# A graph network's edge loop: source buckets rounded up to single tiles, and node weights split in quarters in the loop and behind it

## What is computed

```python
edge_index = jnp.stack([src, dst])
h = jnp.maximum(_layernorm(x), 0.0)
# first layer, row = src, col = dst
edge_feature = silu(edge_rbf @ We1 + be1) @ We2 + be2     # 20625 x 512
msg = edge_feature * h[col]
agg = segment_sum(msg, row, num_segments=625)
x = x + h + (silu(agg @ Wn1 + bn1) @ Wn2 + bn2)
...
# later layers use the same edges, summed by either end, as dense 625 x 625 sums
```

## Time and profile before

| what | value |
|---|---|
| median of 3 runs (lowest, highest) | 1288.35 us (1287.68, 1288.88) |
| profiled execution | 1288.21 us |
| its span on the core | 1286.5 us |
| mean granted clock of TensorE | 0.966 of full speed |
| busy: PE / DVE / ACT / POOL | 93% / 66% / 53% / 37% of the span |

### The profile page before, as it was taken

One profiled execution on the slowest core, in us unless ns is written; L12 is line 12 of the kernel. 1 busy time (PEld: TensorE's weight loads), 2 busy tenths in 40 slices (PEclk: granted clock), 3 DMA queues, 4 the chain that ended last, 5 costly groups with the idle time before them and its releaser, 6 DMA issues.

```text
span 1286.5 us, 21145 instructions
## 1 busy us (share of the span) xinstructions
PE 1200.5 (93%) x6356; PEld 1000.9 (78%) x6356; DVE 855.2 (66%) x1433; ACT 684.9 (53%) x1349; POOL 469.6 (37%) x570
## 2 busy tenths in 40 slices
PE   6989799999999999999999999977879999897687
PEld 4668688888888888888888888867668798876576
DVE  8676377777777777777777777764655171453752
ACT  3475576666666667666666666664423141313241
POOL 2002555555555555555555555613211020221200
PEclk9989899999999999999999999997989999998978
DMA  5533522222222222222222222211001020111101
GB/s 209 210 132 140 207 82 75 71 80 82 80 78 74 74 82 82 79 73 72 82 82 80 78 70 79 80 35 42 1 34 66 1 82 16 39 61 33 42 1 40
DMA packets 27295, 97.22 MB, mean 76 GB/s; under 512 B 6541, under 2 KB 6791, under 8 KB 22906
## 3 DMA queue, kind: packets, MB, share of 16 engines
q0 software_dynamic: 19040, 55.73, 14.5%
q1 hardware_dynamic: 8218, 40.98, 8.8%
HBM read 87.83 MB, written 8.85 MB: 75 GB/s over the span
## 4 chain that ended last, share of the span: by engine, by line
PE 84%; DVE 8%; ACT 4%; issue 3%; DMA 1%; POOL 0%; DVEq 0%; SPq 0%; ACTq 0%
PE ps L821 12%; PE ps L820 12%; PE ps L822 12%; PE ps L813 9%; PE ps L814 9%; PE ps L815 9%; PE ps L914 3%; PE ps L915 3%; PE ps L827 3%; PE ps L828 3%; PE ps L866 2%; PE ps L919 2%; PE ps L854 1%; PE ps L1045 1%; DVE zb_lo L1534 1%
## 5 line engine op out<-in xcount | busy, mean ns | idle before, releaser
L820 PE MATMUL ps<-we_hi,s_hi 128*128 128x512 f32 x680 | 276.7, 407 | 1.8 <-ACT ps L642 1.8
L821 PE MATMUL ps<-we_lo,s_hi 128*128 128x512 f32 x680 | 269.8, 397 | 0.0
L822 PE MATMUL ps<-we_hi,s_lo 128*128 128x512 f32 x680 | 268.1, 394 | 0.0
L483 POOL DMA_INDIRECT xg<-h_dram,node_picks x170 | 178.1, 1048 | 99.2 <-POOL node_picks L473 67.9
L477 POOL DMA_INDIRECT rbf<-in_edge,edge_picks x170 | 175.3, 1031 | 51.8 <-issue 28.6
L639 ACT ACTIVATE m_hi<-msg 128x512 fp32r<-128x512 f32 x170 | 107.6, 633 | 146.9 <-DVE msg L1374 146.9
L1367 DVE TENSOR_TENSOR s_lo<-s,s_hi 128x1024 fp32r<-128x1024 f32 x85 | 104.2, 1226 | 82.9 <-ACT s_hi L633 82.9
L1379 DVE TENSOR_TENSOR m_lo<-msg,m_hi 128x512 fp32r<-128x512 f32 x170 | 117.8, 693 | 58.6 <-ACT m_hi L639 58.6
L822 PEld LDWEIGHTS ps<-we_hi,s_lo 128*128 128x128 f32 x680 | 127.6, 188 | 31.1
L820 PEld LDWEIGHTS ps<-we_hi,s_hi 128*128 128x128 f32 x680 | 128.0, 188 | 26.2 <-issue 2.0
L821 PEld LDWEIGHTS ps<-we_lo,s_hi 128*128 128x128 f32 x680 | 128.8, 189 | 23.0
(11 more groups left out here) (254 smaller groups left out, 2584.6 us busy)
## 6 DMA issues: line engine op xcount, KB each, us to landing
stage<-in_fold_a SPq DMA_DIRECT2D x6, 1024.0 KB, 5.7
stage<-in_fold_b SPq DMA_DIRECT2D x6, 1024.0 KB, 8.6
fold_dram<-folded SPq DMA_DIRECT2D x6, 1024.0 KB, 5.6
wstage<-fold_dram SPq DMA_DIRECT2D x6, 1024.0 KB, 5.0
w_raw<-in_nodew SPq DMA_DIRECT2D x3, 1024.0 KB, 11.0
wstage<-in_selfw SPq DMA_DIRECT2D x3, 1024.0 KB, 4.8
rbf<-in_edge,edge_picks POOLq DMA_INDIRECT x170, 2.7
xg<-h_dram,node_picks POOLq DMA_INDIRECT x170, 3.5
```

The lines of the kernel that those rows point to most:

```text
L483: pool.indirect_dma_start(xg[t.slot][:, j], None, h_dram, bass.IndirectOffsetOnAxis(ap=node_picks[t.slot][:, j:j + 1], axis=0)).then_inc(x ...
L820: pe.matmul(outp, lh, rh, start=False, stop=False, skip_group_check=True)
L821: pe.matmul(outp, lh, rl, start=False, stop=False, skip_group_check=True)
L822: return pe.matmul(outp, ll, rh, start=False, stop=False, skip_group_check=True)
```

## The change

The buckets are rounded up to single tiles of 128 slots. TILES = (20625 + 5 * 127) // 128 = 166, so 83 steps. The even part of each bucket's tiles goes, as pairs, first; the odd tiles left over (at most five) are put behind, from position `solo_at`, at step 80 (SOLO) or later. Steps 80, 81 and 82 may then hold two tiles of different buckets, so each of their tiles has its own sum (banks 5 and 7 for the aggregate, 6 and 0 for the pairs) and its own flush: 86 flushes in all. `whole(c)` counts the flushes before step c, and waits in these steps are on those counts. The sort gets the operations that put the last odd tile of a bucket at its place (`limit`, `jump`, an additional pass over `rank`), and the bucket table has nine passes instead of four.

The node weights are no longer split in the last three steps. w[0] is split by quarters (128 x 512) in steps 1, 2, 80 and 81 on ACT and one step later on DVE, with a semaphore of its own for its transfer. w[1] and w[2] are split whole behind the loop: on ACT after the five copies of the turned aggregate, on DVE after the five low parts. TensorE waits for w[0] before the aggregate is turned, and for the other two before `mlp2`.

The diff without declarations, in which lines of context are left out too:

```diff
@@ -28,8 +28,11 @@
 PAIR = 2 * P
-STEPS = (E + C * (PAIR - 1)) // PAIR
-TILES = 2 * STEPS
+TILES = (E + C * (P - 1)) // P
+STEPS = TILES // 2
+SOLO = STEPS - (C + 1) // 2
+FLUSHES = 2 * STEPS - SOLO
+WEIGHT_CHUNKS = {1: 0, 2: 1, SOLO: 2, SOLO + 1: 3}
...
@@ -107,6 +110,11 @@
+
+def whole(c):
+    return c + max(0, c - SOLO)
...
@@ -355,10 +371,17 @@
-        WEIGHTS = ((we2_hi, we2_lo, we2_raw), (we1_hi, we1_lo, we1_raw),
-                   *((w_hi[i], w_lo[i], w_raw[i]) for i in range(3)))
+        WEIGHTS = ((we2_hi, we2_lo, we2_raw), (we1_hi, we1_lo, we1_raw))
+        NODE_WEIGHTS = len(WEIGHTS) + len(WEIGHT_CHUNKS)
+        def scattered(eng, t):
+            if t.reg is None and t.c > SOLO:
+                eng.wait_ge(scat_mm, 2 * whole(t.c - 1))
+            else:
+                t.wait(eng, scat_mm, 2, -2)
...
@@ -398,13 +421,14 @@
             for i in range(3):
-                sp.dma_start(w_raw[i][:].rearrange("p k f -> p (k f)"), a["nodew"][i]).then_inc(node_weights_in, 16)
+                sp.dma_start(w_raw[i][:].rearrange("p k f -> p (k f)"), a["nodew"][i]).then_inc(
+                    first_weights_in if i == 0 else node_weights_in, 16)
-            sp.wait_ge(flushed, STEPS)
+            sp.wait_ge(flushed, FLUSHES)
...
@@ -571,10 +595,7 @@
                 for i in range(start, end):
-                    if i < 2:
-                        act.wait_ge(edge_weights_in, 32)
-                    else:
-                        act.wait_ge(node_weights_in, 48)
+                    act.wait_ge(edge_weights_in, 32)
...
@@ -644,7 +665,7 @@
                 act.wait_ge(hots_ready, t.count(3, 1))
-                t.wait(act, scat_mm, 2, -2)
+                scattered(act, t)
...
@@ -656,6 +677,12 @@
             def pairs_high(t):
+                if t.reg is None and t.c >= SOLO:
+                    for j in range(2):
+                        act.wait_ge(scat_mm, 2 * whole(t.c) + 3 + j)
+                        act.wait_ge(flushed, whole(t.c) - 1 + j)
+                        act.activation(pairs_i[j][:, 0:ND], ps[0:NC, 6 - 6 * j, 0:ND], ACT.Copy).then_inc(pairs_out, 1)
+                    return
...
@@ -675,8 +702,10 @@
                     seed(1)
-                if t.reg is None and t.c >= STEPS - 3:
-                    weights_high(t.c - STEPS + 5, t.c - STEPS + 6)
+                if t.reg is None and t.c in WEIGHT_CHUNKS:
+                    k = WEIGHT_CHUNKS[t.c]
+                    act.wait_ge(first_weights_in, 16)
+                    act.activation(w_hi[0][:, k], w_raw[0][:, k], ACT.Copy).then_inc(weights_hi, 1)
...
@@ -697,9 +726,12 @@
-            act.wait_ge(flushed, STEPS)
+            act.wait_ge(flushed, FLUSHES)
+            act.wait_ge(node_weights_in, 32)
+            for i in range(1, 3):
+                act.activation(w_hi[i][:], w_raw[i][:], ACT.Copy).then_inc(weights_hi, 1)
...
@@ -909,6 +941,17 @@
                 pe.wait_ge(oh_src_ready, t.count(1, 1))
+                if t.reg is None and t.c >= SOLO:
+                    pe.wait_ge(agg_flushed, whole(t.c))
+                    for j in range(2):
+                        pe.matmul(ps[0:NC, 5 + 2 * j], oh_src[s][:, j, 0:NC], m_hi[s][:, j], start=True, stop=False)
+                        pe.matmul(ps[0:NC, 5 + 2 * j], oh_src[s][:, j, 0:NC], m_lo[s][:, j],
+                                  start=False, stop=True).then_inc(scat_mm, 1)
+                    pe.wait_ge(pairs_out, whole(t.c))
+                    for j in range(2):
+                        pe.matmul(ps[0:NC, 6 - 6 * j, 0:ND], oh_srcb[s][:, j, 0:NC], oh_dst[s][:, j, 0:ND],
+                                  start=True, stop=True).then_inc(scat_mm, 1)
+                    return
...
@@ -992,10 +1035,10 @@
-            pe.wait_ge(flushed, STEPS)
-            pe.wait_ge(weights_hi, len(WEIGHTS))
-            pe.wait_ge(weights_lo, len(WEIGHTS))
-            turn("aggT", lambda c, k: agg3[:, c, k * P:k * P + P], flushed, STEPS, 0)
+            pe.wait_ge(flushed, FLUSHES)
+            pe.wait_ge(weights_hi, NODE_WEIGHTS)
+            pe.wait_ge(weights_lo, NODE_WEIGHTS)
+            turn("aggT", lambda c, k: agg3[:, c, k * P:k * P + P], flushed, FLUSHES, 0)
...
@@ -1017,6 +1060,8 @@
+            pe.wait_ge(weights_hi, NODE_WEIGHTS + 2)
+            pe.wait_ge(weights_lo, NODE_WEIGHTS + 2)
...
@@ -1236,18 +1281,34 @@
             dve.wait_ge(rank_mm, 2)
-            link(dve.tensor_scalar(total_i[:], ps[:, 0, TOTAL_AT:TOTAL_AT + C], float(PAIR - 1), None, ALU.add))
-            shift_by = PAIR.bit_length() - 1
-            link(dve.tensor_scalar(chunks_i[:], total_i[:], shift_by, None, ALU.logical_shift_right))
-            link(dve.tensor_copy(chunks_f[:], chunks_i[:]))
-            link(dve.tensor_tensor_scan(upto[:], chunks_f[:], zeros5[:], 0.0, ALU.add, ALU.add))
+            link(dve.tensor_scalar(total_i[:], ps[:, 0, TOTAL_AT:TOTAL_AT + C], float(P - 1), None, ALU.add))
+            link(dve.tensor_scalar(tiles_i[:], total_i[:], P.bit_length() - 1, None, ALU.logical_shift_right))
+            dve.tensor_scalar(half_tiles[:, 0], tiles_i[:], 1, None, ALU.logical_shift_right).then_inc(halved, 1)
+            dve.tensor_scalar(half_tiles[:, 1], tiles_i[:], 1, None, ALU.bitwise_and).then_inc(halved, 1)
+            dve.wait_ge(halved, 2)
+            link(dve.tensor_copy(chunks_f[:], half_tiles[:]))
+            for i in range(2):
+                link(dve.tensor_tensor_scan(upto[:, i], chunks_f[:, i], zeros5[:], 0.0, ALU.add, ALU.add))
-            link(dve.scalar_tensor_tensor(out=offset[:], in0=first[0:EP], scalar=float(PAIR), in1=ps[0:EP, 0, RANK_AT:RANK_AT + C],
+            dve.tensor_scalar(limit[:], upto[:, 0], float(PAIR), None, ALU.mult).then_inc(halved, 1)
+            dve.tensor_scalar(solo_at[:], upto[:, 0, C - 1:C], float(SOLO), float(PAIR), ALU.max, ALU.mult).then_inc(halved, 1)
+            dve.wait_ge(halved, 3)
+            dve.scalar_tensor_tensor(out=jump[0][:], in0=first[:, 1], scalar=float(P), in1=limit[:],
+                                     op0=ALU.mult, op1=ALU.subtract).then_inc(halved, 1)
+            link(dve.scalar_tensor_tensor(out=offset[:], in0=first[0:EP, 0], scalar=float(PAIR), in1=ps[0:EP, 0, RANK_AT:RANK_AT + C],
+            dve.wait_ge(halved, 5)
+            dve.tensor_scalar(jump[1][:], jump[0][:], solo_at[:, 0:1], None, ALU.add).then_inc(halved, 1)
-            dve.wait_ge(rows_part, 3 * C + 3)
+            dve.wait_ge(halved, 6)
+            for b in range(C):
+                dve.wait_ge(rows_part, 2 * C + 4 + b)
+                dve.tensor_scalar(member[:, b], rank[:, b], limit[0:EP, b:b + 1], jump[1][0:EP, b:b + 1],
+                                  ALU.is_gt, ALU.mult).then_inc(halved, 1)
+            dve.wait_ge(halved, 6 + C)
+            link(dve.tensor_tensor(rank[:], rank[:], member[:], op=ALU.add))
...
@@ -1299,13 +1360,17 @@
                 dve.wait_ge(consts_ready, 9)
-                link(dve.tensor_scalar(first_tile[:], first[:], 2.0, None, ALU.mult))
-                link(dve.tensor_scalar(bucket_f[0][:], tile_no[:], first_tile[:, 1:2], None, ALU.is_ge))
-                for b in range(2, C):
-                    link(dve.scalar_tensor_tensor(out=bucket_f[(b + 1) % 2][:], in0=tile_no[:], scalar=first_tile[:, b:b + 1],
-                                                  in1=bucket_f[b % 2][:], op0=ALU.is_ge, op1=ALU.add))
-                link(dve.tensor_scalar(tile_base[:], bucket_f[C % 2][:], float(NC), None, ALU.mult))
-                link(dve.tensor_copy(bucket_row[:], bucket_f[C % 2][0:1, 0:TILES:2]))
+                link(dve.tensor_scalar(pairs_end[:], upto[:, 0], 2.0, None, ALU.mult))
+                link(dve.tensor_scalar(solo_tile[:], solo_at[:], 1.0 / P, None, ALU.mult))
+                link(dve.tensor_scalar(solo_end[:], upto[:, 1], solo_tile[:, 0:1], None, ALU.add))
+                link(dve.tensor_scalar(bucket_f[0][:], tile_no[:], solo_tile[:, 0:1], float(1 - C), ALU.is_ge, ALU.mult))
+                ends = [pairs_end[:, b:b + 1] for b in range(C - 1)] + [solo_end[:, b:b + 1] for b in range(C - 1)]
+                for i, end_at in enumerate(ends):
+                    link(dve.scalar_tensor_tensor(out=bucket_f[(i + 1) % 2][:], in0=tile_no[:], scalar=end_at,
+                                                  in1=bucket_f[i % 2][:], op0=ALU.is_ge, op1=ALU.add))
+                bucket = bucket_f[len(ends) % 2]
+                link(dve.tensor_scalar(tile_base[:], bucket[:], float(NC), None, ALU.mult))
+                link(dve.tensor_copy(bucket_row[:], bucket[0:1]))
...
@@ -1393,7 +1458,16 @@
-                b = dve.value_load(bucket_row[0:1, bass.ds(t.count(1), 1)], min_val=0, max_val=C - 1)
+                if t.reg is None and t.c >= SOLO:
+                    buckets = [dve.value_load(bucket_row[0:1, t.count(2, j):t.count(2, j) + 1], min_val=0, max_val=C - 1)
+                               for j in range(2)]
+                    for j, b in enumerate(buckets):
```

(22 more changed lines are left out.)

26 lines of the change are left out of this document (17 added, 9 removed).

## The result

The changed kernel takes 1258.69 us (median; 1257.98 to 1259.49), the kernel before 1288.51 in the same comparison: 0.977 of its time, 95% interval 0.976 to 0.979. The profiled execution took 1257.98 us with a span of 1256.1, 30.4 less than the span before.

A forecast was written before the change was run, and what follows sets the result against it. TensorE, 100% busy in the loop, was taken as the bound. Terms -16.87 (steps), -7.6 (loop end), -0.9 (placing matmuls), +0.3 (start) took 1288.21 us to 1263.2; range 1260.0 to 1268.0.

The forecast's parts named there:

- The pace of a step: In the edge loop, the period of a step was to stay 8.43 us.
- the 0.03 for something unseen: Anywhere in the kernel, a chance of 0.03 for an unforeseen effect, either way.
- Two steps less: In the edge loop, 85 steps become 83, saving 2 x 8.43 = 16.87 us on TensorE's path.
- The end of the loop: From the last but one step to the first aggregate transpose, 31.17 us become 23.6, a gain of 7.6.
- The removed splits: At the loop's end, whole-matrix weight splits cost 11.20 us of waits before the last scatter, all taken as removed.
- The flushes: At the loop's end, flushing by tile on VectorE was to add 3.0 us.
- Rival C: Loop's end: ACT and DVE hand over late for each tile, gain falls from 7.6 to 1, 1270 us; chance 0.06.
- Start: Before step 2: placing matmuls save 0.9 us, the longer sort costs 0.3, together -0.6.
- Behind the loop: After the loop, splitting two whole weight matrices on ACT and DVE was to cost 0 us.
- rival B: Around the last scatter and behind it, TensorE's clock stays up after less idle time, 1260.7 us; chance 0.13.
- Rival A: Behind the loop, splits stretched beside GpSimd end late, second node layer starts 2.5 us later, 1265.7 us; chance 0.14.
- Rival D: In the loop, reading the longer bucket row makes DVE the bound, slower, 1297 us at a 2.6 us read; chance 0.02.

The follow-up runs named there:

- b_pad96: The kernel before with 96 unused bytes a partition ahead of the loop's buffers, as they lie in the changed kernel: 1280.96 us, 0.995 of the kernel before.
- weights-alone kernel: The kernel before with only the weight splits changed (quarters in steps 1, 2, 82, 83, other two matrices behind the loop): 1275.95 us, 0.990.
- a_pad32: The changed kernel with 32 unused bytes ahead of the loop's buffers, 128 bytes behind their place in the kernel before: 1265.96 us.
- a_tail: The changed kernel with VectorE's order at the loop's end rewritten (early number reads, alternating flushes, other banks, moved quarter): 1253.33 us, 0.974 of the kernel before.

## Why the prediction was wrong, point by point

**The pace of a step was taken as unchanged (forecast 8.43, found 8.351; 6.5 us).** This is the step that failed: "the period of a step stays 8.43". I had reasoned that in the loop only TensorE's work counts; it does, but I took the same work to mean the same time, and the change moved the buffers of that work by 96 bytes. Moving them alone gives 8.351 (`b_pad96`). The diff showed it: the tables' widths and the bucket row's are there. None of my cases, nor the 0.03 for something unseen, gave it a price, and from the trace of before alone it had none, in size or in sign: at 64 bytes it would have been 0.

**Two steps less: right.** -16.9, at the pace of before.

**The end of the loop: the mechanism right, a term mis-sized.** The removed splits measured 11.0 alone, against 11.2 less 0.6 for a quarter. The flushes, which I had put at 3.0 and which measured 6.5, were costed by their starts in a row of different operations (0.61, 0.80), and the reads at 0.5; the pairs' own signals and the second read add 3.0. My bound of 4 us for this part ("if the flushes wait for one another twice as long as their sum") held it at 4.5, the value I chose did not. The row for it was at hand: the trace named 21.8 us of issue ahead of the 85 flushes, and I used its mean of 0.26 instead of asking how much of a second read lies behind the first. Rival C had the size of the flushes growing, but by hand-overs with ACT; of those there are none in the rows above, its 1270 was far off, and the waits are VectorE's own. As forecast, TensorE has no idle time within the last step but the one ahead of the last scatter, 5.90 us and not 4.

**Start: -2.4 instead of -0.6.** The transposes of step 0's rows start at 131.05 and not at 131.99. I had forecast 0.6 of this 0.9, for the placing matmuls less the sort; the weights-alone kernel, which has the old sort, is at 131.59, so a part of it may be chance too. The first placing matmul starts at 23.43 without a wait; later ones wait for their one-hots twice, 0.8 us together, and before once, 0.5. Of the rest, 1.2 us come in between the first edge layer of step 0 and that of step 1. These are its first matmuls, before and after:

```profile
137.99 0.55 PE L813 MATMUL ps<-rT_hi,we_hi 128*128 128x256 f32 x1 [2.85 <-DVE rT_lo L1361]
```
```profile
137.06 0.35 PE L845 MATMUL ps<-rT_hi,we_hi 128*128 128x256 f32 x1 [2.85 <-DVE rT_lo L1426]
```

After the same wait TensorE runs at the higher level in one execution and at the lower in the other. It isn't the change: the kernel before with the weights alone has 0.36 here and starts step 2 at 159.97, the changed kernel with 32 bytes more has 0.55 and 160.51. So 1.2 us of the 1.8 that were missing are chance of the execution, and belonged in the range.

**Behind the loop: 0 forecast, -1.1 found, by chance.** ACT's two splits start right behind its copies, as forecast. VectorE's and ACT's rows there:

```profile
849.94 3.72 ACT L734 ACTIVATE w_hi<-w_raw 128x2048 fp32r<-128x2048 f32 x2
...
860.15 0.53 ACT L742 ACTIVATE z<-ps,bn 128x314 f32<-128x314 f32 x1 [4.38 <-DVE s_lo L1541]
```
```profile
851.89 6.68 DVE L1537 TENSOR_TENSOR w_lo<-w_raw,w_hi 128x2048 fp32r<-128x2048 f32 x2 [1.01 <-ACT w_hi L734]
858.49 4.94 DVE L1541 TENSOR_TENSOR s_lo<-z,s_hi 128x314 fp32r<-128x314 f32 x4
```

The two subtractions take 3.34 us each beside GpSimd's addition and 2.29 in the loop, 2.1 more together; I had allowed 2.6. They end at 858.57, 13.0 us behind the first transpose, inside the 14.0. The first four s_lo then take 4.94 us and ACT waits for 4.38. All the same TensorE is busy 13.97 of the 14 us from 851 to 865, at a clock of 1.00: the free banks held. It loses 0.5 us only at the adjacency's transposes.

Against that stands the clock, back at 1.00 from 851 on, where before it was still 0.51 for 3 us. I had reckoned with that in rival B, as a fruit of less idle time, but it isn't one. The padded kernels before, which have the old code here and the same 8.0 us of idle time ahead of the last scatter, show both levels: their first node-layer matmul takes 0.38 us in some and 0.60 in others, and from the first transpose to the second node layer they need 22.7 to 23.2 us in the first case and 24.5 to 24.8 in the second. The kernel before had the lower level in its profiled execution (24.57), the changed one the higher (23.43, and 23.15 to 23.43 in the three kernels with the new splits that had it). The level, 1.6 us, is thus chance of the execution. At the higher level the splits behind the loop cost about 0.4 us against the kernels that don't have them there, which fits the 0.5 lost at the transposes.

The first half of rival B did not come either, since the last scatter still starts at 0.76 us a matmul. Rival A (the splits late, +2.5) stayed away. `a_pad32` does need 25.90 us, but TensorE waits for nothing in its first node layer; it is at the lower level, at which two other kernels with the new splits need 24.43 and 24.50. The 1.0 us more from the second layer's start to the end need no cause in the change either: kernels with the same code there take from 384.5 to 387.1 us.

**Rival D** is refuted by the period: VectorE reads the longer row in each step, and at the same place the step is as long as with the short row (8.351 both).

In the sum: 1263.2, less 6.5 for the pace and 1.8 for the start, plus 3.1 for the end, less 0.1 behind it, is 1257.9, and the profiled execution took 1257.98. The sum closes because its terms are differences of marks; some of them are chance (1.2 us at the start, the level of the clock and the 1.0 behind the loop). Without the shift of the buffers, which nobody had planned, the execution would have come to about 1264.5, inside the range, and that too by luck: the forecast had the end 3.1 us too short and the start 1.8 too long.

## What to carry to other kernels

Where TensorE is the bound and never idle, a change of any table's size moves the buffers behind it and can shift the pace, here by up to 1.7%. Compare the number of matmuls in an equal stretch before crediting code, hold the place fixed when two versions are compared, and try a few paddings at the end of tuning: here 32 bytes were worth as much (11.3 us) as moving the weights' splits (11.0). A flush that is cut in two can cost more than twice as much: count the read of its index, and the wait for its twin's signal, and put another operation between the twins.

## What the runs showed of the hardware

- The pace of the same matmuls, all at the granted clock 1.00, depends on the place of the loop buffers in SBUF: 8.293 to 8.433 us for a step, at places 32 bytes apart, with no rule in six of them. Other code at the same place repeats it (8.351 twice, 8.420 twice, 8.293 twice). Whether TensorE's own reads or the other engines' accesses beside them do it stays open.
- Reading two numbers into VectorE's registers ahead of an operation leaves 0.76 us of idle time; reading one leaves 0.13 in a step written out, and 0.22 to 0.33 in the hardware loop of the kernel before (500 to 520 us).
- Waiting for the signal of one's own preceding operation costs VectorE 0.31 us from start to start at 512 elements (0.92 and not 0.61) and 0.22 at 626 (16-bit; 1.02 and not 0.80). With other work between the two it is gone (`a_tail`).
- After the same wait of 2.85 us TensorE goes on at the higher level in some executions and at the lower in others, 1.2 us apart in this stage. The same holds behind the loop, after the same 8.0 us of idle time: 22.7 to 23.2 us or 24.5 to 24.8 to the second node layer.
